# A token shift of the last two sequences by matmuls instead of a DMA, in the third phase of a one-core language-model tower

## The chip, the cores and the metric

The kernel runs on one core of a Trainium2 chip. The metric is the device time of one execution in microseconds (us), from a program that holds all three phases. Three runs of the kernel before gave a median of 1358.09 us (1357.83 to 1359.99).

## The reference, cut to what matters

The reference computes three blocks one after the other on 8 x 256 tokens of width 256 (2048 in one row for the third block): a tower of four layers, an attention block, and a local-attention block of two layers with a gated feed-forward part. The change lies in the feed-forward part of the third block's second layer:

```python
def shift_token(t):
    t1, t2 = jnp.split(t, 2, axis=-1)
    t2 = jnp.pad(t2, ((0, 0), (1, 0), (0, 0)))[:, :-1]
    return jnp.concatenate([t1, t2], axis=-1)
...
        x = x + o @ wo
        h = shift_token(x)
        mu = h.mean(-1, keepdims=True)
        var = h.var(-1, keepdims=True)
        h = (h - mu) / jnp.sqrt(var + 1e-05) * lg + lb
        h = h @ w1 + b1
        a, g = jnp.split(h, 2, axis=-1)
        h = a * jax.nn.gelu(g, approximate=False)
        x = x + h @ w2 + b2
```

The second half of the columns (128 to 255) of every token is replaced by that of the token before it, and the first token of a sequence gets zeros.

## The kernel before, in words

The residual X lies in SBUF with 128 tokens on the partitions. A unit of work of the third phase is one sequence of 256 tokens (two tiles, t = 0 and 1) in one layer; with 8 sequences and 2 layers there are M = 16 units, 0 to 15. The phase is a software pipeline in steps called `half(h)`: in step h, unit a = h is read in, b = h-1 is projected to q, k and v, c = h-2 is scored, d = h-3 is multiplied with the values, e = h-4 is projected out and normed, f = h-5 runs through w1 and g = h-6 through w2. Each engine has its own `half`, with the order of its work written out by hand; semaphores (`S[...]`) tie the engines together. From step 18 on the earlier stages run dry: in step 18 only units 15 (values), 14 (output projection), 13 and 12 are left, in step 19 units 15, 14 and 13, in step 20 units 15 and 14, in step 21 unit 15.

Every matrix product that needs float32 accuracy is made of three fp32r matmuls (high by high, low by high, high by low). The high half is a ScalarE copy (`hidden_hi`), the low half a subtraction (`hidden_lo`, on GpSimd). One group `hidden_in(f, j, u, b, full)` is 12 matmuls with 256 columns into PSUM bank b of a ring of four: blocks j and j+1 of the gate side (u = 1) or of the other side (u = 0). `hidden_out(f, j, b)` is 6 matmuls; it waits for the low half of block j (`h_split`). High and low halves have three buffers each (HS = 3), so `hidden_hi` of block 3 waits for `hidden_out` of block 0.

The path of unit o between the output projection and w1 goes over these steps:

- `project_out` (TensorE, 24 matmuls), then `add_attention` (VectorE, L2205): X gets the attention output, and `x_mid` is raised.
- `shift(o)` (the sync engine's queue, L1536 and L1537): two DMAs copy X's columns 128 to 255, moved down by one partition, into the buffer xs; the second moves the last row of tile 0 to the first row of tile 1.
- `norm_stats(o)` (VectorE, L2215 to L2226) waits for both DMAs. It stands behind `add_output` of unit o-2 (L2247) in VectorE's order, and ahead of `gated` of unit o-1, blocks 0 to 3 (L2241).
- GpSimd's `rstd`, VectorE's `norm_shift` (L2232), ScalarE's `norm` (L1979 and L1980, reads X and xs), TensorE's `turn_normed` (L1701), ScalarE's `affine` (L1992 and L1993, waits for all low halves of the unit ahead), VectorE's `split_normed` (L2236), and then `hidden_in` of the unit.

At the end of step 18 and after, TensorE's `hidden_in(g, 4, 0, 3, "a_full")` waits for `gated` of blocks 2 and 3, since it writes the bank that they read.

ps_d are the two PSUM banks of the attention scores; the last score is read in step 17. m2 is the buffer of the squares and the sine part of the rotary step; its last use is in step 16.

Of the kernel before, what the change touches and what calls it, by code (L numbers as in the profile page):

```python
# [5 lines left out]
F32 = mybir.dt.float32  # L6
# [3 lines left out]
ALU = mybir.AluOpType  # L10
ACT = mybir.ActivationFunctionType
# [3 lines left out]
P = 128  # L15
# [4 lines left out]
D = 256  # L20
# [1368 lines left out]
def window_phase(nc, sems, X, dram, out, raw, qkv, opening, done):  # L1389
# [5 lines left out]
    L, H, HD, INNER, HID = 2, HEADS3, HD3, HEADS3 * HD3, 682  # L1395
    FC = -(-HID // P)
# [3 lines left out]
    ST = 2  # L1400
    STOK = ST * P
    NSQ = NT // ST
# [8 lines left out]
    with ExitStack() as ctx:  # L1411
        def sb(name, shape, dt=F32):
            return ctx.enter_context(nc.sbuf_tensor("w_" + name, shape, dt))
# [5 lines left out]
        def bank(name, n=1):  # L1419
# [36 lines left out]
        HS = 3  # L1456
        h_hi = sb("h_hi", [P, HS, STOK], F32R)
        h_lo = sb("h_lo", [P, HS, STOK], F32R)
        hres = raw_o.rearrange("p (k c) n -> p k (c n)", k=2)

        ring = bank("ring", 4)
# [6 lines left out]
                 "split_qkv split_o split_2 split_1 tab x0 x0_st x0_mv x0_ve x0_rs t1_full ah_done split1 q_full k_full v_full sq_0 sq_1 "  # L1468
                 "ss_0 ss_1 q_read k_read rota_0 rota_1 sc_done lg_done y0_done ya_done yb_done rn_done kscaled qs_full ks_full qt_done kt_done v_done "
                 "d_full sm_done p_done ri scaled p_full pt_done pv_done ot_h ot_split y_full x_mid shifted_0 shifted_1 st mv ve rs nmr xn "  # L1470
                 "t2_full nf_done split2 g_full gelu_done a_full gated h_hi h_split h_used xb x_out")
        S = {x: sem(x) for x in names.split()}

        def xt(m, t):
# [5 lines left out]
        def real(m):  # L1480

            return 0 <= m < M

        def two(u):

# [8 lines left out]
        def sync(sp):  # L1494
# [35 lines left out]
            def shift(o):  # L1530

                sp.wait_ge(S["x_mid"], o + 1)
                if o >= 2:
                    sp.wait_ge(S["xn"], o - 1)
                xg = X[:, ST * (o % NSQ):ST * (o % NSQ) + ST, :]
                sp.dma_start(xs[1:P, o % 2, :, :], xg[0:P - 1, :, P:D]).then_inc(S[f"shifted_{o % 2}"], 16)  # L1536
                sp.dma_start(xs[0:1, o % 2, 1, :], xg[P - 1:P, 0, P:D]).then_inc(S[f"shifted_{o % 2}"], 16)  # L1537
# [24 lines left out]
            def run():  # L1562

                sp.wait_ge(done["qkv_l"], 8)
                load_1(0)
                last = slice(GT * (NG - 1), GT * NG)
                sp.wait_ge(done["y_added"], NSQ)
                sp.dma_start(out_v[:, last, :], X[:, last, :]).then_inc(S["h_out"], 16)
                for stored in done["stored"]:
                    sp.wait_ge(stored, 32)  # L1570
                sp.wait_ge(S["h_out"], 16)
                shift(0)
                shift(1)
                load_qkv()
                load_ow(1)
                shift(2)
                shift(3)
                shift(4)
                load_1(1)
                shift(5)  # L1580
                shift(6)
                shift(7)
                load_h(8)
                load_h(9)
                shift(8)
                load_h(10)
                shift(9)
                load_h(11)
                shift(10)
                store(8)  # L1590
                load_h(12)
                shift(11)
                store(9)
                load_h(13)
                shift(12)
                store(10)
                load_h(14)
                shift(13)
                store(11)
                load_h(15)  # L1600
                shift(14)
                store(12)
                shift(15)
                store(13)
                store(14)
                store(15)
                sp.wait_ge(S["stored"], 16 * NSQ)
# [3 lines left out]
        def tensor(pe):  # L1611
# [72 lines left out]
            def project_out(o, b):  # L1684
# [9 lines left out]
                        mm = pe.matmul(dst, ot_lo[:, c, tok], wo_hi[:, c, :], start=False, stop=(t == ST - 1 and c == IC - 1), skip_group_check=True)  # L1694
                mm.then_inc(S["y_full"], 1)

            def turn_normed(f, b):
                pe.wait_ge(S["xn"], f + 1)
                for c in range(DC):
                    for t in range(ST):  # L1700
                        mm = pe.transpose(ring[:, RB[b], c * STOK + t * P:c * STOK + (t + 1) * P], xn[:, t, c * P:(c + 1) * P], ident[:, :])  # L1701
                mm.then_inc(S["t2_full"], 1)
# [27 lines left out]
            def half(h, last_output=None):  # L1730
# [42 lines left out]
                if real(g):  # L1773
                    if real(c):
                        pe.wait_ge(S["qt_done"], 2 * c + 2)
                    pe.wait_ge(S["gated"], FC * g + 4)
                    hidden_in(g, 4, 0, 3, "a_full")
                    if real(b):
                        pe.wait_ge(S["k_read"], 2 * b + 1)
                    elif real(c):  # L1780
                        pe.wait_ge(S["kt_done"], 2 * c + 1)
                    pe.wait_ge(S["gated"], FC * g + 2)
                    hidden_out(g, 0, 1)
# [28 lines left out]
                if real(e):  # L1812
                    if real(b):
                        pe.wait_ge(S["qt_done"], 2 * b + 1)
                    elif real(c):
                        pe.wait_ge(S["kt_done"], 2 * c + 2)
                    else:
                        pe.wait_ge(S["gelu_done"], FC * g + 4)
                    project_out(e, 0)
                if real(d):  # L1820
                    values(NU * d + 2)
# [4 lines left out]
                if real(f):  # L1826
                    if real(b):
                        pe.wait_ge(S["k_read"], 2 * b + 2)
                    else:
                        pe.wait_ge(S["gated"], FC * g + 6)  # L1830
                    hidden_in(f, 0, 1, 3, "g_full")
                    if real(e):
                        pe.wait_ge(S["x_mid"], e + 1)
                    else:
                        pe.wait_ge(S["gelu_done"], FC * g + 4)
                    hidden_in(f, 2, 1, 0, "g_full")
                    pe.wait_ge(S["nf_done"], DC * f + DC)
                    hidden_in(f, 4, 1, 2, "g_full")
# [56 lines left out]
        def scalar(act):  # L1895
# [79 lines left out]
            def norm(f):  # L1975
                act.wait_ge(S["nmr"], f + 1)
                act.wait_ge(S["t2_full"], f)
                for t in range(ST):
                    act.activation(xn[:, t, 0:P], xt(f, t)[:, 0:P], ACT.Identity, bias=nmr[:, t:t + 1], scale=rs[:, t:t + 1])  # L1979
                    ins = act.activation(xn[:, t, P:D], xs[:, f % 2, t, :], ACT.Identity, bias=nmr[:, t:t + 1], scale=rs[:, t:t + 1])  # L1980
                ins.then_inc(S["xn"], 1)

            def affine(f, p):
# [121 lines left out]
        def vector(dve):  # L2105
# [104 lines left out]
                    dve.bn_stats(st[:, o % 2, t, 0, :], xt(o, t)[:, 0:P])  # L2210

            def norm_stats(f):
                dve.wait_ge(S[f"shifted_{f % 2}"], 32 * (f // 2 + 1))
                for t in range(ST):
                    ins = dve.bn_stats(st[:, f % 2, t, 1, :], xs[:, f % 2, t, :])  # L2215
                ins.then_inc(S["st"], 1)
                dve.wait_ge(S["st"], f + 1)
                if f:
                    dve.wait_ge(S["nmr"], f)
                for t in range(ST):  # L2220
                    ins = dve.bn_aggr(mv[:, t, :], st[:, f % 2, t, :, :].rearrange("p a b -> p (a b)"))
                ins.then_inc(S["mv"], 1)
                dve.wait_ge(S["mv"], f + 1)
                if f:
                    dve.wait_ge(S["rs"], f)
                dve.tensor_scalar(ve[:, :], mv[:, :, 1], EPS, None, ALU.add).then_inc(S["ve"], 1)  # L2226
# [11 lines left out]
            def gated(f, j, b):  # L2238
# [2 lines left out]
                dve.scalar_tensor_tensor(gate[:, j, :], ring[:, RB[b], j % 2 * STOK:(j % 2 + 1) * STOK], b1_all[:, f // NSQ, 0, j:j + 1], gate[:, j, :],  # L2241
                                         ALU.add, ALU.mult).then_inc(S["gated"], 1)

            def add_output(f, b):
                dve.wait_ge(S["xb"], f + 1)
                dve.wait_ge(S["h_used"], FC * f + FC)
                dve.tensor_tensor(x2(f), ring[:, RB[b], :], x2(f), ALU.add).then_inc(S["x_out"], 1)  # L2247

            def half(h):
# [2 lines left out]
                    norm_shift(f)  # L2252
                if real(b):
                    clamp(b, 0)
                if real(g):
                    gated(g, 4, 3)
                    gated(g, 5, 3)
                if real(b):
                    rotate(b, 1, 0, 2)
                if real(c):  # L2260
# [56 lines left out]
                if real(c):  # L2317
                    inverse_sums(NU * c + 2)
                    soft(H * c + 6)
                if real(f):  # L2320
                    gated(f, 2, 3)
                    gated(f, 3, 3)
                if real(c):
# [45 lines left out]
        def gpsimd(pool):  # L2369
# [49 lines left out]
            def add_bias(f):  # L2419
# [6 lines left out]
                else:  # L2426
# [2 lines left out]
                    pool.wait_ge(S["b2_added"], f - NSQ + 1)  # L2429
                    pool.tensor_tensor(x2(f), x2(f), hres[:, f % 2, :], ALU.add).then_inc(S["xb"], 1)  # L2430

            def half(h):
                a, b, c, d, e, f = h, h - 1, h - 2, h - 3, h - 4, h - 5
                if h == 3:
# [4 lines left out]
                    x0_root(2)  # L2439
                if real(b):  # L2440
                    scale_k(b, 1)
                if real(f):
                    hidden_lo(f, 0)
                if h == 5:
                    lo_2(0)
                if real(f):
                    hidden_lo(f, 1)
                if h == 3:
                    x0_root(3)
# [1 line left out]
                    lo_qkv(2)  # L2451
                if real(c):
                    scale_p(NU * c + 2)
                if real(f):
                    hidden_lo(f, 2)
                if h == 0:
                    x0_root(1)
# [4 lines left out]
                    add_sin(a, 0, 1)  # L2462
                if h == 7:
                    lo_qkv(0)
                if real(f):
                    hidden_lo(f, 3)
                    hidden_lo(f, 4)
                    hidden_lo(f, 5)
# [168 lines left out]
```

## Time and profile before

| | |
|---|---|
| median of 3 runs | 1358.09 us |
| the profiled execution's own time | 1364.02 us |
| its span | 1362.3 us |
| mean granted clock of TensorE | 0.967 of full |
| TensorE matmul busy | 1244.2 us (91%) |
| VectorE, ScalarE, GpSimd busy | 970.2, 923.7, 634.2 us |

The span runs from the first to the last instruction of the core. The granted clock is the share of full speed that TensorE was given; 1.00 is 2.4 GHz and 0.50 is 1.2 GHz. Times of the rows below count from the start of the span, and the second number of a timeline's row is its duration. A number in brackets at the end of a row is the time that the engine stood idle before it, with the engine whose work ended the wait.

### The profile page before, as it was taken

Reading aid. Unit: us, or ns where it says so; the run is one execution under the profiler, and the core shown is the slowest. Engines: PE = TensorE matmul, PEld = TensorE weight load, DVE = VectorE, ACT = ScalarE, POOL = GpSimd, SP = SyncE. Lnnn points to the kernel's source line nnn. Section 1 sums busy time; section 2 is a strip of 40 time slices with the busy share of each in tenths; the row PEclk is TensorE's granted clock in tenths of the full one; section 3 lists DMA queues with packets and bytes.
Section 4 is the critical chain, followed back from the end, with each engine's and each line's share of the span. In section 5 each row is a group of like instructions: output and inputs, shape, how many; then the busy total and the mean of one; then the engine's idle time right before and its main releaser. Section 6 shows DMA issues by size and latency. Waiting matters only on the chain.

```text
span 1362.3 us, 26380 instructions
## 1 busy us (share of the span) xinstructions
PE 1244.2 (91%) x9057; PEld 1065.0 (78%) x9057; DVE 970.2 (71%) x2602; ACT 923.7 (68%) x2023; POOL 634.2 (47%) x697
## 2 busy tenths in 40 slices
PE   2799999999999993899977888999999999999986
PEld 2699888989988993677755566888788888888876
DVE  5767666666667746898786886778787888877532
ACT  2455765565676642889956778788778788888633
POOL 6523421442343214455334566556556566555523
PEclk9799999999999997999987999999999999999988
DMA  7300010010000004000010002000100000000010
GB/s 170 98 1 14 32 33 1 14 64 1 1 1 1 1 0 115 1 17 14 12 65 1 2 5 87 5 6 5 47 5 6 17 4 13 20 21 21 20 32 16
DMA packets 34881, 33.75 MB, mean 25 GB/s; under 512 B 11340, under 2 KB 31424, under 8 KB 34752
## 3 DMA queue, kind: packets, MB, share of 16 engines
q1 hardware_dynamic: 33856, 29.91, 7.2%
q0 software_dynamic: 768, 2.10, 1.0%
q8 instruction: 79, 1.29, 0.4%
q14 instruction: 50, 0.41, 0.1%
q10 hardware_dynamic: 128, 0.04, 0.0%
HBM read 25.75 MB, written 4.19 MB: 22 GB/s over the span
## 4 chain that ended last, share of the span: by engine, by line
PE 41%; ACT 8%; DVE 4%; POOL 3%; issue 3%; DMA 2%; SPq 1%; ACTq 0%; DVEq 0%; POOLq 0%
PE w_ring L1633 2%; PE w_ring L1635 2%; PE w_ring L1634 2%; PE w_ps_p L1663 2%; PE w_ring L1713 2%; PE a_ps L845 2%; PE w_ring L1714 2%; PE w_ring L1715 2%; PE w_ps_a L1681 2%; PE w_ring L1640 2%; DMA w_xs<-X 2%; PE w_ring L1725 2%; PE w_ps_d L1656 1%; PE w_ps_d L1653 1%; PE w_ring L1726 1%
## 5 line engine op out<-in xcount | busy, mean ns | idle before, releaser
L360 ACT ACTIVATE t_gf<-t_ps_f,t_fb_cur 128x512 f32<-128x512 f32 x128 | 87.9, 687 | 166.0 <-PE t_ps_f L280 164.3
L508 DVE TENSOR_TENSOR t_g_lo<-t_gf,t_g_hi 128x512 fp32r<-128x512 f32 x128 | 94.2, 738 | 81.2 <-ACT t_g_hi L362 80.4
L293 PE MATMUL t_ps_o<-t_w_hi,t_g_hi 128*128 128x256 f32 x512 | 145.9, 285 | 0.9 <-DVE t_g_lo L508 0.9
L295 PE MATMUL t_ps_o<-t_w_hi,t_g_lo 128*128 128x256 f32 x512 | 144.9, 283 | 0.0
L294 PE MATMUL t_ps_o<-t_w_lo,t_g_hi 128*128 128x256 f32 x512 | 144.9, 283 | 0.0
L1713 PE MATMUL w_ring<-w_nh,w_w_hi 128*128 128x256 f32 x384 | 114.5, 298 | 12.8 <-DVE w_gate L2241 6.1
L644 POOL TENSOR_TENSOR t_rs<-t_ve,t_neghalf 128x4 f32<-128x4 f32 x32 | 38.5, 1203 | 181.3 <-DVE t_ve L469 180.0
L2196 DVE COPY w_pt<-w_ps_p 128x384 f32<-128x384 f32 x128 | 70.5, 551 | 60.2 <-PE w_ps_p L1663 59.0
L278 PE MATMUL t_ps_f<-t_nh,t_w_hi 128*128 128x512 f32 x256 | 103.5, 404 | 7.9 <-DVE t_nl L607 3.6
L1714 PE MATMUL w_ring<-w_nh,w_w_lo 128*128 128x256 f32 x384 | 109.2, 284 | 0.0
L1715 PE MATMUL w_ring<-w_nl,w_w_hi 128*128 128x256 f32 x384 | 109.1, 284 | 0.0
L2411 POOL TENSOR_TENSOR w_h_lo<-w_gate,w_h_hi 128x256 fp32r<-128x256 f32 x96 | 69.8, 735 | 80.6 <-ACT w_h_hi L2006 80.2
L2395 POOL TENSOR_TENSOR w_m<-w_m 128x512 f32<-128x512 f32 x64 | 85.4, 1334 | 42.7 <-DVE w_m L2153 42.7
L279 PE MATMUL t_ps_f<-t_nh,t_w_lo 128*128 128x512 f32 x256 | 101.8, 398 | 0.0
L293 PEld LDWEIGHTS t_ps_o<-t_w_hi,t_g_hi 128*128 128x128 f32 x512 | 97.8, 191 | 4.9 <-issue 1.3
L280 PE MATMUL t_ps_f<-t_nl,t_w_hi 128*128 128x512 f32 x256 | 100.8, 394 | 0.0
L294 PEld LDWEIGHTS t_ps_o<-t_w_lo,t_g_hi 128*128 128x128 f32 x512 | 98.0, 191 | 2.6
L295 PEld LDWEIGHTS t_ps_o<-t_w_hi,t_g_lo 128*128 128x128 f32 x512 | 98.0, 191 | 0.0
L1633 PE MATMUL w_ring<-qkv_hi,w_ah 128*128 128x512 f32 x192 | 83.4, 434 | 8.4 <-DVE w_al L2135 5.0
L1713 PEld LDWEIGHTS w_ring<-w_nh,w_w_hi 128*128 128x128 f32 x384 | 74.2, 193 | 14.9 <-DVE w_gate L2241 6.7
L362 ACT ACTIVATE t_g_hi<-t_gf 128x512 fp32r<-128x512 f32 x128 | 80.9, 632 | 4.1
L2406 POOL TENSOR_TENSOR w_pr<-w_pr,w_rinv 128x256 f32<-128x256 f32 x64 | 39.3, 613 | 95.2 <-DVE w_rinv L2190 95.2
(290 smaller groups left out, 4375.4 us busy)
## 6 DMA issues: line engine op xcount, KB each, us to landing
t_raw<-in_L_tok_w SPq DMA_DIRECT2D x8, 1024.0 KB
out<-X SPq DMA_DIRECT2D x14, 256.0 KB, 2.1
raw<-in_L_ffn_wqkv SPq DMA_DIRECT2D x2, 1536.0 KB, 6.8
raw<-in_L_ffn_w SPq DMA_DIRECT2D x4, 682.0 KB, 5.0
w_raw_o<-out SPq DMA_DIRECT2D x8, 256.0 KB, 3.1
w_xs<-X SPq DMA_DIRECT2D x16, 127.0 KB
w_raw<-in_L_ffn_w SPq DMA_DIRECT2D x2, 640.0 KB
t_raw_d<-in_L_tok_D SPq DMA_DIRECT2D x4, 256.0 KB
```

Source lines behind the costliest of these rows:

```text
L278: pe.matmul(ps_f[:, j % 2, :], w1_hi[:, c, col], nh[1][:, c, :], start=(c == 0), stop=False)
L279: pe.matmul(ps_f[:, j % 2, :], w1_lo[:, c, col], nh[1][:, c, :], start=False, stop=False)
L280: mm = pe.matmul(ps_f[:, j % 2, :], w1_hi[:, c, col], nl[1][:, c, :], start=False, stop=(c == DC - 1))
L293: pe.matmul(out, g_hi[:, j % 4, tok], w2_hi[:, j, :], start=(j == 0 and t % 2 == 0), stop=False, skip_group_check=True)
L294: pe.matmul(out, g_hi[:, j % 4, tok], w2_lo[:, j, :], start=False, stop=False, skip_group_check=True)
L295: mm = pe.matmul(out, g_lo[:, j % 4, tok], w2_hi[:, j, :], start=False, stop=(j == FC - 1 and t % 2 == 1), skip_group_check=True)
L360: act.activation(gf[:, j % 2, :], ps_f[:, j % 2, :], ACT.Gelu, bias=fb_cur[:, j:j + 1]).then_inc(pf_free, 1)
L508: dve.tensor_tensor(g_lo[:, j % 4, :], gf[:, j % 2, :], g_hi[:, j % 4, :].bitcast(F32), ALU.subtract).then_inc(g_split, 1)
L1633: pe.matmul(ring[:, RB[b], :], ah[:, c, tok], qkv_hi[:, c, cols], start=(c == 0), stop=False)
L1713: pe.matmul(dst, w1_hi[:, c, u, cols], nh[:, c, :], start=(j % 2 == 0 and c == 0), stop=False, skip_group_check=True)
L1714: pe.matmul(dst, w1_lo[:, c, u, cols], nh[:, c, :], start=False, stop=False, skip_group_check=True)
L1715: mm = pe.matmul(dst, w1_hi[:, c, u, cols], nl[:, c, :], start=False, stop=(j % 2 == 1 and c == DC - 1), skip_group_check=True)
```

## The change

For units 14 and 15 (`by_matmul`) the two DMAs of `shift` go away. In their place TensorE multiplies X's columns 128 to 255 with a 0/1 matrix `down` (row p takes row p-1) and adds tile 0's last row to tile 1 with a second 0/1 matrix `carry`, in plain float32, into a bank of ps_d. VectorE's statistics and ScalarE's norm read those banks. GpSimd makes the two matrices in m2, in step 17, between `hidden_lo(12, 0)` and `hidden_lo(12, 1)`. In steps 19 to 21 `hidden_in(g, 4, 0, ...)` goes to bank 0 instead of bank 3 and waits only for the gelu; `project_out` of unit 15 and the gate side of the next unit, which use bank 0 after it, wait for `gated` of blocks 4 and 5 in return. The low halves of the last unit's hidden blocks (f = 15) move from GpSimd to VectorE.

```diff
+        down, carry = m2[:, 0, 0:P], m2[:, 0, P:2 * P]
...
+        def by_matmul(m):
+            return M - 2 <= m < M
...
                 load_h(15)
-                shift(14)
                 store(12)
-                shift(15)
                 store(13)
...
+            def shift_rows(o):
+                pe.wait_ge(S["turner"], 3)
+                pe.wait_ge(S["x_mid"], o + 1)
+                pe.wait_ge(S["sm_done"], H * M)
+                xg = X[:, ST * (o % NSQ):ST * (o % NSQ) + ST, P:D]
+                dst = ps_d[:, o % 2, 0:STOK].rearrange("p (t d) -> p t d", d=P)
+                pe.matmul(dst, down[:, :], xg, start=True, stop=False, skip_group_check=True)
+                pe.matmul(dst[:, 1, :], carry[:, :], xg[:, 0, :], start=False, stop=True, skip_group_check=True).then_inc(S["moved"], 1)
...
-                    pe.wait_ge(S["gated"], FC * g + 4)
-                    hidden_in(g, 4, 0, 3, "a_full")
+                    if real(d):
+                        pe.wait_ge(S["gated"], FC * g + 4)
+                        hidden_in(g, 4, 0, 3, "a_full")
+                    else:
+                        pe.wait_ge(S["gelu_done"], FC * g + 4)
+                        hidden_in(g, 4, 0, 0, "a_full")
...
+                    elif real(d):
+                        pe.wait_ge(S["gelu_done"], FC * g + 4)
                     else:
-                        pe.wait_ge(S["gelu_done"], FC * g + 4)
+                        pe.wait_ge(S["gated"], FC * g + 6)
                     project_out(e, 0)
...
                     else:
-                        pe.wait_ge(S["gelu_done"], FC * g + 4)
+                        pe.wait_ge(S["gated"], FC * g + 6)
+                    if by_matmul(e):
+                        shift_rows(e)
                     hidden_in(f, 2, 1, 0, "g_full")
...
-                    ins = act.activation(xn[:, t, P:D], xs[:, f % 2, t, :], ACT.Identity, bias=nmr[:, t:t + 1], scale=rs[:, t:t + 1])
+                    rows = ps_d[:, f % 2, t * P:(t + 1) * P] if by_matmul(f) else xs[:, f % 2, t, :]
+                    ins = act.activation(xn[:, t, P:D], rows, ACT.Identity, bias=nmr[:, t:t + 1], scale=rs[:, t:t + 1])
...
             def norm_stats(f):
-                dve.wait_ge(S[f"shifted_{f % 2}"], 32 * (f // 2 + 1))
+                if by_matmul(f):
+                    dve.wait_ge(S["moved"], f - (M - 2) + 1)
+                else:
+                    dve.wait_ge(S[f"shifted_{f % 2}"], 32 * (f // 2 + 1))
...
+            def hidden_lo(f, j):
+                dve.wait_ge(S["h_hi"], FC * f + j + 1)
+                dve.tensor_tensor(h_lo[:, j % HS, :], gate[:, j, :], h_hi[:, j % HS, :].bitcast(F32), ALU.subtract).then_inc(S["h_split"], 1)
...
+                if g == M - 1:
+                    hidden_lo(g, 1)
+                    hidden_lo(g, 2)
                 if real(g):
-                    gated(g, 4, 3)
-                    gated(g, 5, 3)
+                    gated(g, 4, 3 if real(d) else 0)
+                    gated(g, 5, 3 if real(d) else 0)
+                if g == M - 1:
+                    hidden_lo(g, 3)
+                    hidden_lo(g, 4)
+                    hidden_lo(g, 5)
...
                 if real(f):
+                    if f == M - 1:
+                        hidden_lo(f, 0)
                     gated(f, 2, 3)
                     gated(f, 3, 3)
...
+            def row_matrices():
+
+                pool.wait_ge(S["rota_0"], 2 * M)
+                pool.wait_ge(S["rota_1"], 2 * M)
+                pool.memset(m2[:, 0, 0:2 * P], 0.0).then_inc(S["turner"], 1)
+                pool.wait_ge(S["turner"], 1)
+                for x, base in ((down, 1), (carry, 1 - P)):
+                    pool.affine_select(out=x, in_=x, compare_op=ALU.not_equal, fill=1.0, base=base,
+                                       pattern=[[-1, P]], channel_multiplier=1).then_inc(S["turner"], 1)
...
-                if real(f):
+                if 0 <= f < M - 1:
                     hidden_lo(f, 0)
...
+                if h == M + 1:
+                    row_matrices()
```

## Rows read from the trace of the kernel before

**Rows 1.** The page: granted clock of TensorE in 40 slices of the span.
```profile
PEclk9799999999999997999987999999999999999988
```
**Rows 2.** The chain that ended last, in order of time: start us, us, what.
```profile
1295.62 7.71 DMA w_xs<-X
...
1318.69 7.91 DMA w_xs<-X
```
**Rows 3.** Timeline of VectorE, steps 18 to 21.
```profile
1299.48 0.69 DVE L2247 TENSOR_TENSOR X<-w_ring,X 128x512 f32<-128x512 f32 x1 [0.83 <-PE w_ring L1727]
1303.35 0.49 DVE L2215 BATCH_NORM_STATS2 w_st<-w_xs 128x6 f32<-128x128 f32 x2 [3.18 <-DMA w_xs<-X]
...
1304.26 0.88 DVE L2241 SCALAR_TENSOR_TENSOR w_gate<-w_ring,w_b_all,w_gate 128x256 f32<-128x256 f32 x2
...
1305.38 0.87 DVE L2241 SCALAR_TENSOR_TENSOR w_gate<-w_ring,w_b_all,w_gate 128x256 f32<-128x256 f32 x2
...
1323.29 0.69 DVE L2247 TENSOR_TENSOR X<-w_ring,X 128x512 f32<-128x512 f32 x1 [4.87 <-PE w_ring L1727]
1326.63 0.49 DVE L2215 BATCH_NORM_STATS2 w_st<-w_xs 128x6 f32<-128x128 f32 x2 [2.65 <-DMA w_xs<-X]
...
1357.70 0.69 DVE L2247 TENSOR_TENSOR X<-w_ring,X 128x512 f32<-128x512 f32 x1 [3.60 <-PE w_ring L1727]
```
**Rows 4.** Timeline of TensorE: rows ahead of which it stood idle.
```profile
1140.26 0.66 PE L1640 MATMUL w_ring<-w_ident,w_m 128*128 128x128 f32 x4 [1.83 <-DVE w_gate L2241]
...
1282.89 0.52 PE L1663 MATMUL w_ps_p<-w_ident,w_pr 128*128 128x128 f32 x3 [1.52 <-DVE w_pt L2196]
...
1306.30 0.58 PE L1713 MATMUL w_ring<-w_nh,w_w_hi 128*128 128x256 f32 x1 [2.99 <-DVE w_gate L2241]
...
1317.44 0.36 PE L1713 MATMUL w_ring<-w_nh,w_w_hi 128*128 128x256 f32 x1 [0.84 <-DVE w_nl L2236]
...
1329.25 0.58 PE L1713 MATMUL w_ring<-w_nh,w_w_hi 128*128 128x256 f32 x1 [2.13 <-DVE w_gate L2241]
...
1339.20 0.35 PE L1713 MATMUL w_ring<-w_nh,w_w_hi 128*128 128x256 f32 x1 [3.52 <-DVE w_nl L2236]
...
1347.44 0.39 PE L1713 MATMUL w_ring<-w_nh,w_w_hi 128*128 128x256 f32 x1 [0.85 <-DVE X L2247]
...
1351.50 0.39 PE L1713 MATMUL w_ring<-w_nh,w_w_hi 128*128 128x256 f32 x1 [0.97 <-DVE w_gate L2241]
```
**Rows 5.** Stretches: us, busy us (instructions) of PE, PEld, DVE, ACT, POOL, granted clock, DMA.
```profile
1140.20:1144.00 3.80, 3.74 (x30) 3.21 (x31) 3.73 (x14) 2.55 (x8) 3.42 (x5) 1.00 0.01 2
1306.00:1310.00 4.00, 3.70 (x17) 3.70 (x18) 1.42 (x4) 1.96 (x5) 1.37 (x3) 0.50 0.02 6
1318.00:1323.00 5.00, 5.00 (x46) 4.97 (x44) 0.42 (x2) 2.52 (x6) 0.00 (x0) 1.00 0.05 13
1329.25:1332.50 3.25, 3.25 (x15) 3.25 (x16) 0.33 (x2) 1.66 (x5) 1.40 (x3) 0.50 0.00 0
```
**Rows 6.** The chain in order of time: two score matmuls in plain float32.
```profile
1276.01 0.43 PE w_ps_d L1656 x4
```
**Rows 7.** Timeline of GpSimd, steps 17 and 20.
```profile
1279.42 1.43 POOL L2411 TENSOR_TENSOR w_h_lo<-w_gate,w_h_hi 128x256 fp32r<-128x256 f32 x2
...
1281.38 1.04 POOL L2407 TENSOR_TENSOR w_pr<-w_pr,w_rinv 128x512 f32<-128x512 f32 x1
...
1333.76 2.12 POOL L2411 TENSOR_TENSOR w_h_lo<-w_gate,w_h_hi 128x256 fp32r<-128x256 f32 x3 [3.11 <-ACT w_h_hi L2006]
```
**Rows 8.** Groups of GpSimd by form: busy us, mean ns of one, idle before.
```profile
L2498 POOL MEMSET w_mask<- 128x384 f32 x1 | 0.4, 417 | 0.0
L2500 POOL TENSOR_SCALAR_AFFINE_SELECT w_ident<-w_ident 128x128 f32<-128x128 f32 x1 | 0.3, 328 | 0.0
```
**Rows 9.** A group of VectorE by form, with the same columns.
```profile
L2201 DVE TENSOR_TENSOR w_ot_lo<-w_ps_a,w_ot_hi 128x256 fp32r<-128x256 f32 x64 | 26.4, 413 | 3.3 <-ACT w_ot_hi L1973 3.2
```
**Rows 10.** Timeline of ScalarE: the last of the norm's four instructions, unit 14.
```profile
1307.90 0.48 ACT L1980 ACTIVATE w_xn<-w_xs,w_nmr,w_rs 128x128 f32<-128x128 f32 x1
```

More of the change, by code:

```diff
@@ L1470, in window_phase @@
                  "d_full sm_done p_done ri scaled p_full pt_done pv_done ot_h ot_split y_full x_mid shifted_0 shifted_1 st mv ve rs nmr xn "
-                 "t2_full nf_done split2 g_full gelu_done a_full gated h_hi h_split h_used xb x_out")
+                 "moved turner t2_full nf_done split2 g_full gelu_done a_full gated h_hi h_split h_used xb x_out")
         S = {x: sem(x) for x in names.split()}
@@ L2212, in norm_stats @@
             def norm_stats(f):
-                dve.wait_ge(S[f"shifted_{f % 2}"], 32 * (f // 2 + 1))
+                if by_matmul(f):
+                    dve.wait_ge(S["moved"], f - (M - 2) + 1)
+                else:
+                    dve.wait_ge(S[f"shifted_{f % 2}"], 32 * (f // 2 + 1))
                 for t in range(ST):
-                    ins = dve.bn_stats(st[:, f % 2, t, 1, :], xs[:, f % 2, t, :])
+                    rows = ps_d[:, f % 2, t * P:(t + 1) * P] if by_matmul(f) else xs[:, f % 2, t, :]
+                    ins = dve.bn_stats(st[:, f % 2, t, 1, :], rows)
                 ins.then_inc(S["st"], 1)
@@ L2445, in half @@
                     lo_2(0)
-                if real(f):
+                if h == M + 1:
+                    row_matrices()
+                if 0 <= f < M - 1:
                     hidden_lo(f, 1)
@@ L2453, in half @@
                     scale_p(NU * c + 2)
-                if real(f):
+                if 0 <= f < M - 1:
                     hidden_lo(f, 2)
@@ L2464, in half @@
                     lo_qkv(0)
-                if real(f):
+                if 0 <= f < M - 1:
                     hidden_lo(f, 3)
```

## Prediction

> **What bounds the kernel now.** I read the page first. TensorE is the busiest engine over the whole span, and its granted clock is high except in a few slices, the last two among them [rows 1]. A mean over 1362 us says nothing of the last 60, so I went to the chain that ended last. There two pieces stand out near the end, and both are the shift's DMA: 7.71 us from 1295.62 and 7.91 us from 1318.69 [rows 2]. VectorE's timeline shows how much of them is uncovered: it had finished the addition ahead of the statistics at 1300.17 and 1323.98, and then stood idle 3.18 and 2.65 us for xs [rows 3]. TensorE's timeline shows the price one step later. The group that waits for `gated` of blocks 2 and 3 started after 2.99 us of idleness at 1306.30, and after 2.13 us at 1329.25 [rows 4]. The windows show a second price: behind both gaps the clock was 0.50 (1.2 GHz), 17 matmuls in 3.70 us and 15 in 3.25 us, some 0.217 us each, against 46 in 5.00 us or 0.109 at 1.00 (2.4 GHz) [rows 5]. With the small steps between groups I count 0.115 us for a matmul at full clock, so 1.4 us for a group of 12. So the end is a chain in which VectorE, late for the DMA, holds TensorE.
>
> **The change part by part.** I walk the end of the schedule in the new order and name where each milestone falls, beside where it fell.
>
> *GpSimd's matrices.* A memset of 256 columns lies under the 0.417 us of 384 columns, say 0.31; two selects at 0.33 make 0.65; together 0.95 us [rows 8]. They stand ahead of one of the two low halves that began at 1279.42 and of the scaling of the probabilities that ended at 1282.42 [rows 7]. The scaling now ends at 1283.37. Behind it on GpSimd wait later low halves with slack; behind the scaling waits TensorE's next transposition, which ran at 1282.89 [rows 4]. VectorE had released that one; GpSimd had been done 0.4 us earlier. So TensorE starts at 1283.45, 0.56 us late, and since it works without a gap from there to the stretch of interest, all 0.56 us arrive there. Bounds: 0 if the three instructions cost under 0.4 us, 1.0 if they cost 1.4.
>
> *The shift matmuls.* The trace has no float32 matmul with a 128x128 weight in this phase. The nearest are the two score matmuls with 64-row weights that ran side by side: 0.43 us for 256 columns [rows 6]. I take 0.43 for `down`, half for `carry` and 0.15 for switching, 0.8 us a unit. The lower bound is 0.17, as if they were of the fast form at 0.115 for 256 columns; the upper is 1.3, the two score matmuls one after the other and a carry at the same rate. They stand behind the first gate group and need `x_mid`, which is there. The result is ready some 5 us before VectorE asks for it, so the statistics no longer wait, and the only cost is 0.8 us of TensorE in each of steps 18 and 19. That the statistics and the norm read PSUM instead of xs I count as nothing: no row shows these forms, and even 0.1 us for each of the two in a chain would be 0.2 a unit. On the sync engine's queue four DMA issues go away; behind them stand only stores, which wait for later additions anyway.
>
> *Step 18 to 19.* The addition of unit 12 ended at 1300.17 [rows 3]; it now ends at 1300.17 + 0.56 + 0.8 = 1301.5. Statistics take 0.91 us (1303.35 to 1304.26) [rows 3], done at 1302.45. TensorE runs three groups of 12 in a row, since the third has bank 0: to 1303.0, 1304.35 and 1305.75. Before, the third began at 1306.30 at half clock. VectorE's gating of blocks 2 and 3 (0.88) ends at 1305.35. The norm begins at 1305.45 and takes 1.65 (its fourth instruction began at 1307.90, [rows 10]), to 1307.1. TensorE's `hidden_out` of blocks 0 to 2 and the four transpositions go to 1308.25; block 3 and the 24 matmuls of `project_out` to 1311.7. The last high half follows the norm and `hidden_out` 2 at about 1308.25, and GpSimd's three low halves at 0.71 each [rows 7] run from 1307.6 to 1309.7. From that point to the next unit's first matmul is `affine` and `split_normed`: the low halves ended at 1335.88 and the matmul began at 1339.20, 3.32 us [rows 4, 7]. So unit 14 starts in w1 at 1313.05 instead of 1317.44: 4.4 us gained.
>
> *Step 19 to 20.* From there to the addition of unit 13 lie 12 + 24 + 12 matmuls and the shift: 1323.29 - 1317.44 = 5.85 before, 6.65 now, so the addition is at 1319.6 to 1320.3 (1323.98 before). The same walk as above: statistics done 1321.2, three groups to 1324.55, gating of block 3 to 1324.15, norm to 1325.95, `hidden_out` 2 done 1326.65, low halves to 1328.55, unit 15 in w1 at 1331.9 instead of 1339.20: 7.3 us gained. TensorE stands idle from 1327.9, 4.0 us where it was 3.52, so I leave the slow matmuls behind that gap as they were.
>
> *Steps 20 and 21.* From 1339.20 to 1347.44 nothing changes, so the first group of the last a side starts at 1340.15. Before, the third group began 4.06 us after the first, at 1351.50 [rows 4], waiting for the gating; now the three run through to 1344.4, and `hidden_out`'s 36 matmuls take 4.15 more if no low half is late. VectorE's low half is 0.41 us by the nearest form [rows 9] against 0.71 on GpSimd. Block 3 is the tight one: its high half follows `hidden_out` 0 at 1345.1, 0.42 us on ScalarE, then 0.41, ready at 1346.15, while TensorE comes to it at 1346.5. So the last addition starts at 1348.7 instead of 1357.70 [rows 3]. What follows it, stores and the wait for them, stays as it is.
>
> The shared port speaks against that move. VectorE's `split_normed` of 512 elements waits behind GpSimd at times, but GpSimd's last work, the bias and residual of unit 15, ends near 1331.2, so nothing contends with the low halves. The Trainium skill, "SBUF — State Buffer", section "Who interferes with whom", says that only the port pair shared by VectorE and GpSimd contends and that an instruction with two SBUF inputs is locked out for the whole of the other's; by that rule, too, the move costs nothing where GpSimd is idle. No row here shows a low half on VectorE.
>
> **The sum.** 4.4 (step 19) + 2.9 (step 20) + 1.7 (the tail) = 9.0 us. It is made against the profiled execution, whose span is 1362.3 and whose own time is 1364.02, 5.9 us above the median. I take the saving over as it is: 1358.1 - 9.0 = 1349.1 us.
>
> **The rivals.**
>
> *A new gap lowers the clock (chance 0.35).* With the matrices, TensorE's idle time before 1283.45 is 1.52 + 0.56 = 2.08 us. In this trace idle stretches of 1.83 and 1.52 left the clock at 1.00, and the one of 2.13 brought 0.50 [rows 4, 5]. 2.08 lies between these, so I can't tell. A stretch at half clock costs 0.1 us a matmul, 15 to 28 of them, so 1.5 to 2.8, say 2.1: 1351.2 us. The Trainium skill, "TensorE: Matmul & The Clock Gate", section "What's actually happening", makes the slow clock the default, which activity releases; by it a longer gap anywhere can cost a slow stretch. That is what the rows after the gaps show.
>
> *The gain is only partly there (0.1).* If unit 14's statistics were held by something else that was late as well (the addition of unit 12, GpSimd's root), only a part of the first 4.4 comes: some 1353 us. Against it: the row before the statistics names the DMA alone, and its idle time is 3.18 us of a DMA of 7.71 [rows 2, 3].
>
> *The DMA was hidden, no change (0.03).* Then TensorE's gaps came from elsewhere and the time stays 1358. The released bank 0 would still save the wait, so it needs both to fail.
>
> *Slower (0.02).* If the clock fell at 1283.45 and stayed at 1.2 GHz through the dense stretch up to 1301, the 17 us of work there would cost up to 17 more: 1366. It decides from some 90 slow matmuls on (9.0 / 0.1); the longest slow stretch here, from 1306.30, holds under 30.
>
> **How the numbers follow.** My forecast has a chance of 0.5 and, by the bounds of the shift (2 x -0.63 and 2 x +0.5), the matrices (-0.56, +0.4) and the clock behind the last gap (-1.6 to +1.2), its own range is 1345.7 to 1351.7 with all bounds at their ends at once; I take 1346.2 to 1351.5. With the clock's rival (1351.2, and up to 2 us of the same bounds on top) and half of the partial one it becomes 1346.2 to 1353.3. 0.2%, or 2.7 us, is about what a measurement of this kernel can tell from no change: faster means below 1355.4. Faster 0.94, same 0.04, slower 0.02.
>
> **What the new profile would show.** No DMA into xs after 1270; VectorE's statistics of units 14 and 15 right behind L2247, with no wait; three groups of 12 on TensorE without idleness ahead of the third; a granted clock of 1.00 between 1303 and 1327; unit 14 in w1 4.4 us and unit 15 7.3 us earlier; the last stage from L2247 to L2247 about 8.6 us long instead of 10.3. Wrong it would be if the float32 shift took over 1.5 us, if idleness ahead of the transposition near 1283 were followed by a clock of 0.50, or if VectorE, which now does gating and low halves, came late for TensorE in the last 9 us.

## The result, and the profile after

The changed kernel has a median of 1354.53 us against 1359.38 us before, 20 runs each. The ratio is 0.9964, with a 95% interval of 0.9951 to 0.9976: faster by 4.9 us (3.3 to 6.7). I had forecast 9.0. The direction is right; the size is not, and 1354.5 lies above the top of my range. The median of before is itself 1.3 us above the one of three runs that I had added the forecast to (1358.09), so of the 5.4 us between 1349.1 and 1354.5 the gain that is missing is 4.1. A ratio here is always that of a kernel's times to those of before, measured beside it.

The profiled execution has a span of 1351.0 us, 11.3 less than that of before. Not all of it is the change's: TensorE's last transposition ahead of its idle stretch in step 18 ended at 1276.27, and at 1281.37 before, so 5.1 us had come apart earlier, in code that both kernels share. To leave that out I take in every profile the time from the end of this transposition to the end of the last matmul, and call it the count. The count was 76.23 us before and is 70.04 now, so this stretch gained 6.2 us.

VectorE's timeline answers to [rows 3]:

```profile
1297.10 0.69 DVE L2276 TENSOR_TENSOR X<-w_ring,X 128x512 f32<-128x512 f32 x1 [0.86 <-PE w_ring L1739]
1297.71 0.49 DVE L2240 BATCH_NORM_STATS2 w_st<-w_ps_d 128x6 f32<-128x128 f32 x2
...
1316.14 0.69 DVE L2276 TENSOR_TENSOR X<-w_ring,X 128x512 f32<-128x512 f32 x1 [5.64 <-PE w_ring L1739]
1316.75 0.49 DVE L2240 BATCH_NORM_STATS2 w_st<-w_ps_d 128x6 f32<-128x128 f32 x2
```

Both statistics follow the addition with no idle time ahead of them; the waits of 3.18 and 2.65 us are gone, as is the DMA. TensorE's timeline, the rows that answer to [rows 4]:

```profile
1278.33 0.33 PE L1666 MATMUL w_ps_p<-w_ident,w_pr 128*128 128x128 f32 x1 [2.06 <-POOL w_pr L2445]
...
1297.85 0.39 PE L1725 MATMUL w_ring<-w_nh,w_w_hi 128*128 128x256 f32 x1
...
1309.53 0.36 PE L1725 MATMUL w_ring<-w_nh,w_w_hi 128*128 128x256 f32 x1 [1.01 <-DVE w_nl L2261]
...
1316.89 0.39 PE L1725 MATMUL w_ring<-w_nh,w_w_hi 128*128 128x256 f32 x1 [0.85 <-DVE X L2276]
...
1328.49 0.55 PE L1725 MATMUL w_ring<-w_nh,w_w_hi 128*128 128x256 f32 x1 [3.66 <-DVE w_nl L2261]
...
1337.70 0.39 PE L1725 MATMUL w_ring<-w_nh,w_w_hi 128*128 128x256 f32 x1 [0.85 <-DVE X L2276]
```

The gaps ahead of the third groups (2.99, 2.13 and 0.97 us) are gone. The first gap has grown from 1.52 to 2.06 us and is now ended by GpSimd. The stretches behind the gaps, in the columns of [rows 5]:

```profile
1278.30:1282.60 4.30, 4.28 (x25) 3.71 (x26) 1.69 (x5) 1.64 (x6) 0.66 (x1) 0.63 0.00 0
...
1297.90:1302.40 4.50, 4.50 (x38) 4.50 (x39) 3.02 (x12) 1.87 (x5) 2.52 (x4) 1.00 0.19 62
1328.50:1333.50 5.00, 5.00 (x23) 5.00 (x24) 0.00 (x0) 0.84 (x2) 0.00 (x0) 0.50 0.00 0
1333.50:1337.70 4.20, 3.35 (x27) 3.14 (x26) 0.69 (x1) 1.68 (x4) 0.00 (x0) 0.93 0.00 0
```

The three groups of step 19 run at 1.00 (2.4 GHz), where the third ran at 0.50 before. But the clock is down to 0.63 in the stretch behind the first gap, and behind the last gap it is 0.50 (1.2 GHz) for 5.0 us and 0.93 in the next 4.2. Behind the first gap the kernel before ran at full speed; its window there:

```profile
1282.90:1286.00 3.10, 3.09 (x27) 2.57 (x27) 1.77 (x6) 1.23 (x5) 0.20 (x1) 1.00 0.00 0
```

Put side by side, in us, from the starts and ends in TensorE's timelines (the forecast's column is worked out from the milestones of the prediction; e1 is an experiment below):

| stretch on TensorE | before | forecast | after | e1 |
|---|---|---|---|---|
| end of the transposition to end of `project_out` 14 | 10.82 | 11.38 | 12.81 | 10.92 |
| to the first group behind the addition of unit 12 | 8.03 | 8.83 | 8.77 | 8.78 |
| to unit 14 in w1 | 17.22 | 11.5 | 11.68 | 11.68 |
| to the first group behind the addition of unit 13 | 6.59 | 7.3 | 7.36 | 7.36 |
| to unit 15 in w1 | 15.17 | 11.55 | 11.60 | 11.63 |
| to the first group behind the addition of unit 14 | 8.24 | 8.24 | 9.21 | 8.21 |
| to the end of the last matmul | 10.16 | 8.5 | 8.61 | 8.61 |
| count | 76.23 | 67.3 | 70.04 | 67.19 |

Five of seven stretches are within 0.2 us of the forecast. The first is 1.4 us over it and the sixth 1.0, and in both the granted clock is low.

### The profile page after: what moved, and what is told of

It is laid out like the page before. It is cut to its first block, busy times and chain, and to the rows that moved or that the text cites. A ratio compares the mean times of both kernels' runs of the same rounds, so it can differ in the third digit from the quotient of the medians.

```text
span 1351.0 us, 26400 instructions
## 1 busy us (share of the span) xinstructions
PE 1238.0 (92%) x9065; PEld 1059.3 (78%) x9065; DVE 972.1 (72%) x2608; ACT 923.1 (68%) x2023; POOL 630.2 (47%) x694
## 4 chain that ended last, share of the span: by engine, by line
PE 41%; ACT 8%; DVE 4%; POOL 3%; issue 3%; SPq 1%; DMA 1%; ACTq 0%; DVEq 0%; POOLq 0%
PE w_ring L1725 3%; PE w_ps_p L1666 3%; PE w_ring L1726 3%; PE w_ring L1727 2%; PE w_ring L1636 2%; PE w_ring L1638 2%; PE w_ring L1637 2%; PE w_ps_a L1684 2%; PE a_ps L845 2%; PE w_ring L1643 2%; PE w_ring L1737 2%; PE w_ps_d L1659 1%; PE w_ring L1738 1%; PE w_ring L1739 1%; PE w_ps_d L1656 1%
## 5 line engine op out<-in xcount | busy, mean ns | idle before, releaser
L2449 POOL TENSOR_TENSOR w_h_lo<-w_gate,w_h_hi 128x256 fp32r<-128x256 f32 x90 | 65.7, 736 | 64.1 <-ACT w_h_hi L2027 64.0
L1666 PE MATMUL w_ps_p<-w_ident,w_pr 128*128 128x128 f32 x384 | 67.6, 286 | 14.8 <-POOL w_pr L2445 7.8
```

The source lines that it names most:

```text
L1666: mm = pe.transpose(ps_p[:, 0, b * P:(b + 1) * P], pr[:, k % SLOTS, b * P:(b + 1) * P], ident[:, :])
```

## The experiments

My theory after the result: the schedule does what I worked out, and two stretches at half clock take back 2.4 us of it; the one in step 18 comes with the gap that GpSimd's matrices widen. The rival: the matrices and the shift cost more than I gave them, and the clock is by the way. Counts are of one profiled execution each, so I give the ratio of the times beside them.

**e1: the matrices later.** They move to a place where GpSimd stood idle.

```diff
-                if h == M + 1:
-                    row_matrices()
                 if 0 <= f < M - 1:
                     hidden_lo(f, 1)
...
                 if 0 <= f < M - 1:
                     hidden_lo(f, 2)
+                if h == M + 1:
+                    row_matrices()
```

> The changed kernel with the 0/1 matrices made one place later on GpSimd, behind hidden_lo(12, 2), where it stood idle. I count from the end of TensorE's last transposition ahead of the gap (1281.37 before, 1276.27 after the change) to the end of the last matmul: 76.2 us before, 70.0 after. Theory (the gap made by the matrices brought the slow clock): the idle time is 1.5 us again, the clock behind it stays at 1.00, and the count falls by 2.0 us to 68.0. Rival (the schedule itself costs more than I worked out, the clock has no part): only the 0.54 us of delay come back, 69.5. Time: about 2 us (0.15%) below the changed kernel by the theory, 0.5 by the rival.

Measured: 0.9939 (0.9920 to 0.9957), so 8.3 us under before, against 4.9 for the changed kernel; the two intervals overlap by 0.0006. The count is 67.19. TensorE's gap and the window behind it:

```profile
1279.19 0.30 PE L1666 MATMUL w_ps_p<-w_ident,w_pr 128*128 128x128 f32 x1 [1.52 <-DVE w_pt L2217]
```

```profile
1279.10:1284.00 4.90, 4.80 (x41) 4.31 (x42) 2.75 (x8) 3.04 (x11) 1.11 (x4) 1.00 0.00 0
1328.00:1332.00 4.00, 3.96 (x21) 3.99 (x22) 0.00 (x0) 0.84 (x2) 0.00 (x0) 0.60 0.00 0
1332.00:1336.30 4.30, 3.45 (x29) 3.25 (x28) 0.69 (x1) 1.68 (x4) 0.00 (x0) 0.98 0.00 0
```

The gap is 1.52 us again and the clock behind it 1.00. The first stretch falls from 12.81 to 10.92, 1.9 us as the theory said, where the rival had 0.54. The rest (1.0 us) is the stretch behind the last gap: 3.68 us of idleness where the changed kernel has 3.66, but fewer slow matmuls behind it. I had not foreseen that, and the matrices' place does not explain it.

**e2: the matrices alone.** The kernel before, with `row_matrices` where the change has it and no reader.

```diff
+                if h == M + 1:
+                    row_matrices()
                 if real(f):
                     hidden_lo(f, 1)
```

> The kernel before with nothing but the matrices on GpSimd in the place where the change puts them; nobody reads them. Theory: idle time of 2.1 us ahead of the transposition, a slow stretch behind it, the count of 76.2 us becomes 78.2, and the time is 2 us (0.15%) above before. Rival: 0.5 us more only, 76.7, with a clock of 1.00 there.

Measured: 1.0014 (1.0000 to 1.0028), 1.9 us slower, as the theory had it for the time, though the interval begins at no change. The window behind the widened gap (2.05 us idle) and the one behind TensorE's wait for the gating of unit 14, with that wait's row:

```profile
1278.80:1282.00 3.20, 3.16 (x18) 2.43 (x19) 1.59 (x5) 0.42 (x2) 0.67 (x1) 0.64 0.00 0
1325.60:1329.40 3.80, 3.78 (x32) 3.78 (x33) 0.94 (x3) 2.51 (x7) 2.25 (x5) 1.00 0.00 0
```

```profile
1325.62 0.39 PE L1714 MATMUL w_ring<-w_nh,w_w_hi 128*128 128x256 f32 x1 [1.99 <-DVE w_gate L2242]
```

The slow stretch in step 18 came: `project_out` of unit 14 ended 12.75 us after the transposition (10.82 before). But the count is 75.67, not 78.2. Behind the wait that had been 2.13 us [rows 4] and was 1.99 here, the clock stayed at 1.00. So one slow stretch came and another went, and the count of a single execution does not decide; its first stretch does, and the time agrees. The same wait was 2.01 us in e8 (below), and there the clock fell, as behind the 2.13 us of before:

```profile
1329.75 0.58 PE L1727 MATMUL w_ring<-w_nh,w_w_hi 128*128 128x256 f32 x1 [2.01 <-DVE w_gate L2262]
```

```profile
1329.75:1333.00 3.25, 3.25 (x15) 3.25 (x16) 0.32 (x2) 1.65 (x4) 1.40 (x3) 0.50 0.00 0
```

**e5: the gap filled, the delay left.** 12 matmuls into an idle bank, read by nobody, ahead of the transposition.

```diff
+                if d == M - 1:
+                    filler(12)
                 if real(d):
                     turn_p(H * d + 4)
```

> The changed kernel, matrices in the place where the change has them, with 12 matmuls that nobody reads in TensorE's idle time ahead of the transposition that waits for GpSimd (2.06 us after the change). It parts the delay from the clock. Theory (delay 0.54 us, clock 1.43): the clock stays at 1.00 behind it and the count, 70.0 after the change and 67.2 with the matrices late, becomes 67.7, or 68.7 where the last gap brings the longer slow stretch. Rival (the matrices cost by their delay alone): 70 or more.

Measured: count 67.69, clock 1.00 in the 4.8 us behind the gap. This parts the two: with the delay kept and the clock kept up, the first stretch is 11.49, 0.6 above e1, and the other 1.3 us of the changed kernel's 12.81 are the clock. The sixth stretch, behind the last gap, is 8.27 for 9.21, another 0.9 of the count that I had not aimed at. The time is 0.9959 (0.9942 to 0.9976), 5.6 us under before, less than the 8.5 of the count; the interval does not part it from the changed kernel. So this split is shown in the trace, not in the time.

**e9 and e10: the changed kernel twice more.**

> The changed kernel as it is, profiled once more, to see whether its slow stretches come in every execution. Theory: 2.06 us of idleness ahead of the transposition and a stretch at 0.50 behind it again; behind the last long gap 3.7 us idle and at least one slow stretch; count between 69.0 and 70.1. Rival (the slow stretch behind the matrices was chance): 1.00 there and a count of 67.7 to 68.7.

> The same once more, for a third execution: theory and rival as for the run ahead of it.

Measured: counts 70.28 (0.18 above what I expected) and 69.98 (70.04 the first time), idle times 2.07 and 2.06 us. The windows behind the first and the last gap, of e10:

```profile
1281.20:1284.40 3.20, 3.19 (x20) 2.63 (x21) 1.69 (x5) 0.54 (x2) 0.64 (x1) 0.68 0.00 0
1331.30:1337.00 5.70, 5.70 (x27) 5.70 (x28) 0.00 (x0) 1.09 (x3) 0.00 (x0) 0.50 0.00 0
```

So both slow stretches came in three executions of three (and the first in e2 and e7 too, five of five with the matrices in that place and no filling, against none in the eight profiles with 1.52 or 1.53 us of idleness there). The one in step 18 is a cost of this schedule, not chance.

**e3: the last gap filled.** As e1, with 26 matmuls that nobody reads ahead of unit 15's first group in w1.

```diff
                     hidden_out(g, 3, 1)
+                if g == M - 2:
+                    filler(26)
```

> As e1, and 26 matmuls of 256 columns that nobody reads in TensorE's last long gap, ahead of unit 15's first group in w1 (3.66 us idle after the change, followed by slow matmuls). Theory: they take 3.0 us of the gap, the clock stays at 1.00 behind it, the 48 matmuls to the next addition take 6.6 us instead of 9.2, and the count is about 65.4. Rival (what is slow there is not the clock but low halves or transfers): no gain over e1, 68.0, or a loss where the filling comes in the way of unit 15.

Measured: count 65.72. The window from unit 15's first group in w1 on:

```profile
1331.40:1337.30 5.90, 5.89 (x48) 5.69 (x48) 0.00 (x0) 2.52 (x6) 0.00 (x0) 1.00 0.01 3
```

All 48 matmuls at 1.00; the sixth stretch is 6.74 us, against 9.21 after the change, 8.24 before and 8.21 in e1. The start of unit 15 did not move. So the clock behind that gap costs 1.5 to 2.5 us. The time is 0.9937 (0.9918 to 0.9956), against 0.9939 of e1: the 1.5 us are below what six runs can tell.

**e6, e7 and e8: one part alone each.** e6 has only the new bank and its waits; e7 only the shift, with its matrices; e8 only the last low halves on VectorE. Two of the edits by which the parts were taken out, the shift in e6 and e8, the bank in e7 and e8:

```diff
         def by_matmul(m):
-            return M - 2 <= m < M
+            return False
...
-                    if real(d):
-                        pe.wait_ge(S["gated"], FC * g + 4)
-                        hidden_in(g, 4, 0, 3, "a_full")
-                    else:
-                        pe.wait_ge(S["gelu_done"], FC * g + 4)
-                        hidden_in(g, 4, 0, 0, "a_full")
+                    pe.wait_ge(S["gated"], FC * g + 4)
+                    hidden_in(g, 4, 0, 3, "a_full")
```

> Only the new bank for the third group of matmuls and its waits; shift by DMA, low halves on GpSimd, no matrices. Theory: the statistics still wait some 3 us for the DMA, but TensorE runs the third group in that time, so the gaps split and the clock stays up; unit 14 in w1 33.0 us after the end of the transposition (36.1 before, 31.4 in e1), unit 15 at 53.1 (57.8 before), the count 70.5 (76.2 before). Rival (the shift's DMA was the whole of it): under 1 us of gain.

> Only the shift by matmuls with its matrices in the place of the change; third group in bank 3 behind the gating as before, low halves on GpSimd. Theory: 2.0 us lost at the start to the matrices (0.54 delay, the rest clock), 0.65 a shift, no wait of the statistics; unit 14 in w1 at 33.6, count 72.2, so 4 us under before. Rival (the bank was the whole of it): count 76 to 78.

> Only the last unit's low halves on VectorE. Theory: with the third group still waiting for the gating, VectorE's first low half stands ahead of the gating of blocks 2 and 3 and gives back what the quicker low halves bring: the last stage (from the first group behind the addition of unit 14 to the last matmul, 10.16 us before, 8.61 after the change) takes 9.7 to 10.2. Rival (the 1.55 us of the last stage are all VectorE's quicker low half): 8.6.

| | count | unit 14, unit 15 in w1 | last stretch | ratio (95%) |
|---|---|---|---|---|
| before | 76.23 | 36.07, 57.83 | 10.16 | 1 |
| e6 bank alone | 70.54 | 33.17, 52.52 | 8.92 | 0.9963 (0.9948 to 0.9977) |
| e7 shift alone | 72.46 | 34.21, 54.07 | 10.17 | 0.9968 (0.9952 to 0.9983) |
| e8 low halves alone | 76.13 | 36.27, 58.01 | 9.84 | 0.9998 (0.9978 to 1.0018) |

Over the whole count the parts do not add up: alone they bring 5.7, 3.8 and 0.1 us, together 6.2. The bank alone brings 5.7 us of count though the statistics still wait for the DMA: TensorE does its third group in that time, and the gaps that are left are too small to bring the slow clock (0.88 and 1.56 us). The shift alone brings 3.8 with the loss in step 18 in it (2.1 us, a first stretch of 12.90 for 10.82); without that it would be some 5.9 by my estimate, as much as the bank. The low halves alone bring 0.3 in the last stretch, 0.1 in the count.

**e4: the low halves of unit 14 on VectorE too.** As e1, with `hidden_lo` moved for the last two units.

```diff
-                if g == M - 1:
+                if g >= M - 2 and real(g):
                     hidden_lo(g, 3)
                     hidden_lo(g, 4)
                     hidden_lo(g, 5)
```

> As e1, and the low halves of unit 14 on VectorE too. Theory: GpSimd's three low halves in a row (0.73 each) hold the affine step of unit 15; on VectorE (0.41) the last is ready some 1 us sooner, the last long gap is 2.7 us, and the count falls from 68.0 to 67.0, more if the slow stretch shortens. Rival: VectorE comes late for the gating of blocks 4 and 5 or GpSimd's additions lock it out, count 68 or more.

Measured: count 68.65, unit 15 in w1 at 50.60 (50.37 in e1), ratio 0.9948 (0.9930 to 0.9967). The rival was right in that unit 15 did not start sooner. Its count of 68 or more has another source: of the 1.46 us above e1 only 0.23 are the later start, and 1.23 are the stretch behind the last gap (9.44 for 8.21, with a clock of 0.50 for the first 5.1). VectorE's and GpSimd's timelines show which half of it:

```profile
1326.97 3.06 DVE L2271 TENSOR_TENSOR w_h_lo<-w_gate,w_h_hi 128x256 fp32r<-128x256 f32 x3 [0.49 <-ACT w_h_hi L2027]
```

```profile
1326.71 1.28 POOL L2465 TENSOR_TENSOR X<-X,w_b_all 128x512 f32<-128x512 f32 x1 [4.11 <-ACT w_xn L2001]
1328.14 1.27 POOL L2468 TENSOR_TENSOR X<-X,w_raw_o 128x512 f32<-128x512 f32 x1
```

Three low halves that take 0.42 us each when alone took 3.06, and they lie under GpSimd's two additions: singly the first took 1.30 us and the second 1.50, and each ended 0.3 us after one of the additions. Rid of its own low halves, GpSimd began these additions at once, and they ran into VectorE's.

**e11: as e4, with GpSimd's additions held back.**

```diff
+                if e == M - 1:
+                    pool.wait_ge(S["h_split"], FC * (M - 1))
                 if real(e):
                     add_bias(e)
```

> As e4 (matrices late, low halves of unit 14 on VectorE too), but GpSimd begins the bias and residual of unit 15 only when the low halves of unit 14 are done. In e4 VectorE's last three low halves took 3.06 us in a row, while GpSimd's two additions ran beside them. Theory (the additions locked VectorE out of its second input): the three take about 1.6 us with the waits for ScalarE, unit 15 starts in w1 at 49.2 us on my count instead of 50.7, and the count is 65.7 to 66.7 by the clock behind the gap. Rival (VectorE was late for its own work): 50.5 or more, and no gain.

Measured: count 66.54, unit 15 in w1 at 49.72. VectorE:

```profile
1325.65 0.83 DVE L2271 TENSOR_TENSOR w_h_lo<-w_gate,w_h_hi 128x256 fp32r<-128x256 f32 x2 [0.49 <-ACT w_h_hi L2027]
1326.73 0.42 DVE L2271 TENSOR_TENSOR w_h_lo<-w_gate,w_h_hi 128x256 fp32r<-128x256 f32 x1 [0.25 <-ACT w_h_hi L2027]
...
1329.21 1.24 DVE L2261 TENSOR_TENSOR w_nl<-w_gate,w_nh 128x512 fp32r<-128x512 f32 x1 [2.05 <-ACT w_nh L2014]
```

The three now take 1.5 us with ScalarE's waits in them, 0.42 us each. This confirms the contention. The Trainium skill, "SBUF — State Buffer", section "Who interferes with whom", has it as an exclusive lock on the port pair that the two engines share, held for whole instructions; the numbers of e4 and e11 agree. The gain is 0.65 us at unit 15's start, not the 1.2 I had expected, since `split_normed` now runs beside the held additions, as in e1: 1.24 us here and 1.13 there, against 0.69 in e4, where it ran alone. The ratio is 0.9942 (0.9920 to 0.9964), no better than e1's.

**e12: e11 with the last gap filled.**

> As e11 with 14 matmuls that nobody reads in the last long gap. Theory: no slow stretch from the transposition on, 6.7 us from unit 15's first matmul in w1 to the next addition's release, count 64.4 to 64.8, and the quickest of all kernels here by some 11 us (0.8%) against before. Rival: the time does not follow the count, since other slow stretches of other executions take its place.

Measured: count 65.06, the lowest here, with the clock at 1.00 from unit 15's first group on (48 matmuls in 5.73 us of a window of 5.80). But the ratio is 0.9942 (0.9921 to 0.9963): 7.9 us, not 11. The rival is nearer. The time of the whole kernel does not show the last 2 us of the count.

## Why the prediction was right or wrong

*What bounds the end* was right: VectorE's wait for the DMA, then TensorE's wait for the gating, then the clock. The first two are gone, and with them the slow clock behind both waits for the gating. The stretches from the additions to the units' starts in w1 came within 0.2 us of the schedule (11.68 for 11.5, 11.60 for 11.55). The starts themselves moved less than the 4.4 and 7.3 us that I named, by 2.8 and 5.6 on the count, since the loss in step 18 lies ahead of both; in e1 they moved by 4.7 and 7.5, and the count of e1 is the one that I had forecast (67.19 for 67.3).

*The matrices.* Their own cost was right. GpSimd's timeline after the change has the memset start at 1275.01 and the next low half at 1275.98, 0.97 us for 0.95:

```profile
1275.01 0.31 POOL L2474 MEMSET w_m<- 128x256 f32 x1
1275.47 0.54 POOL L2477 TENSOR_SCALAR_AFFINE_SELECT w_m<-w_m 128x128 f32<-128x128 f32 x2 [0.15 <-POOL w_m L2474]
1275.98 0.72 POOL L2449 TENSOR_TENSOR w_h_lo<-w_gate,w_h_hi 128x256 fp32r<-128x256 f32 x1
```

The gap grew by 0.54 us for my 0.56. What I priced at nothing in the forecast and at 2.1 us in a rival with a chance of 0.35, the slow clock behind it, came every time and cost 1.45 us: 1.99 us of the first stretch less the 0.54 of delay. e1, which narrows the gap, and e5, which fills it, both bring the full clock back.

*The shift matmuls.* 0.8 a unit was near: 0.74 and 0.77 in the table. The chain has them at 0.43 and 0.22:

```profile
1291.77 0.43 PE w_ps_d L1706 x2
1292.20 0.22 PE w_ps_d L1707 x2
```

*The step that failed* is the treatment of TensorE's clock, which the sum left where it was: "so I leave the slow matmuls behind that gap as they were" (measured 9.21 for 8.24, 0.97 us more, filled 6.74 in e3), together with the choice of the case without a fall at 1283 as the likeliest. Together 2.4 us of the 2.8 by which the count of 70.04 misses the 67.2 that a gain of 9.0 means. The mechanism of the schedule was right; the term for the clock was mis-sized. I had the 1.0 us within a bound of the last gap (1.2) and 2.1 for the rival, but both stood beside the sum and not in it. The range up to 1353.3 had room for the two; past its top the time was carried by the 1.3 us that the median of before lies higher and by 1.3 us of gain that the count does not miss. The 1.45 us in step 18 come from the gap that the matrices widened. What made the stretch behind the last gap longer stays open: e1 and e5 had the same gap and the shorter stretch. As for those other 1.3 us (4.1 short in time, 2.8 in the count), the prediction took the saving of the profiled execution, 5.9 us slower than the median, over to the median "as it is"; no run shows whether that step lost them.

*The bank.* I folded it into the schedule and named no price of its own. e6 shows that it carries as much as the shift.

*The low halves.* The last stretch was forecast at 8.5 and came at 8.61, 1.55 less than before. Most of it is the bank's: alone it brings 1.24 (e6), VectorE's quicker low halves alone 0.3 (e8), and here the two add up.

*What stays open.* The count fell by 6.2 us and the time by 4.9 (3.3 to 6.7). That is within the interval, but in nine of the eleven timed comparisons with before, the changed kernel's among them, the time gained less than the count: 5.6 for 8.5 in e5, 7.9 for 11.2 in e12. A reading that fits is that the profiled execution of before, with three slow stretches, was worse than its usual one; e2, which kept one of these waits at 1.99 us, had no slow stretch there. Against it speaks e8, whose schedule is that of before up to unit 15's part in w1: it had all three again, and a count of 76.13. I did not profile the kernel before again, so why the time gained less than the count is not shown.

## What to carry to other kernels

When work moves onto an engine in a busy step, look at what stands next in its order, and at the idle time of TensorE that hangs on it: half a microsecond of delay cost two here, because the gap that it widened was followed by the slow clock. One place later it was free within 0.1 us (a first stretch of 10.92 for 10.82 in e1). Two parts that ease the same wait don't add up; a bank of PSUM that lets TensorE do its next group during the wait brought, by itself, about what the whole changed kernel did (0.9963 and 0.9964), without matmuls or matrices for the shift. And an engine that is relieved of work starts its next instruction sooner, which may be just the one that locks another engine out.

## What the runs showed that I had not expected

- In these profiles TensorE's clock was at 0.50 for a time behind each idle stretch of 2.05 to 2.07 us in step 18 (five of five), and stayed at 1.00 behind 1.52 us there. Behind TensorE's wait for the gating of unit 14 it stayed at 1.00 after 1.99 us in e2 and was at 0.50 after 2.01 us in e8.
- Behind the same last gap (3.66 to 3.70 us) the cost differed: the 48 matmuls up to the next addition and the addition took 9.21, 9.23 and 9.28 us in the three executions of the changed kernel and 9.10 in e6, but 8.21 in e1 and 8.27 in e5. No run shows what decides between the two.
- ScalarE's norm of 128 columns took 442 ns from PSUM and 478 ns from SBUF; VectorE's statistics 286 and 281.
